# Perceiver block on one core: keys' chain between the query projections, queries' chain between the levels

## What is computed

```python
x = x + xattn(layernorm(x), ctx)
x = x + attn(layernorm(x))
x = x + ffn(layernorm(x))
```

```python
q, k, v = (silu(short_conv(h @ W.T, conv)) for q, k, v)
beta = sigmoid(h @ Wb.T)
q, k = q / |q|, k / |k|                 # per token and head
T = inverse(I + tril(beta * k @ k.T, -1))
delta = tril(q @ k.T) @ (T @ (beta * v))
o = p0 * fir3(v) + p1 * fir15(v) + p2 * fir63(v) + p3 * delta + p4 * v
return rmsnorm(o) @ Wo.T                # p0..p4: gate softmax per head
```

## Time and profile before

| | us |
|---|---|
| runs | 483.11, 485.64, 489.86 |
| median | 485.64 |
| the profiled execution | 488.1 |
| its span, first to last instruction | 486.3 |

### The profile page before, as it was taken

How to read it: one execution, slowest core, us unless ns; L and a number is a source line. 1 busy time by engine, 2 the same in 40 slices (tenths; PEclk the granted TensorE clock), 3 DMA queues, 4 the chain that set the end, 5 groups by cost and what they waited for, 6 DMA issues and landing times.

```text
span 486.3 us, 8120 instructions
## 1 busy us (share of the span) xinstructions
PE 447.0 (92%) x3154; PEld 291.8 (60%) x3154; DVE 317.7 (65%) x596; ACT 164.3 (34%) x208; POOL 78.6 (16%) x77
## 2 busy tenths in 40 slices
PE   2998997899998997899999979999998899999985
PEld 1953343445563574658776437887445688888862
DVE  5441225467983889997748774552214999999955
ACT  1102110245730010112223153204005788788630
POOL 1000000000004580002552110047200000000061
PEclk9999998899998599999968999999999999999998
DMA  8999939433040505007300020037707999999535
GB/s 324 430 427 427 425 137 306 156 81 93 1 173 19 156 21 157 3 1 276 160 3 0 2 86 0 1 128 223 235 1 292 375 402 395 373 410 405 219 112 169
DMA packets 17937, 92.41 MB, mean 190 GB/s; under 512 B 3424, under 2 KB 5104, under 8 KB 10736
## 3 DMA queue, kind: packets, MB, share of 16 engines
q1 hardware_dynamic: 14880, 78.82, 42.9%
q10 hardware_dynamic: 1488, 8.93, 5.3%
q0 software_dynamic: 1536, 4.20, 2.6%
HBM read 82.25 MB, written 12.08 MB: 194 GB/s over the span
## 4 chain that ended last, share of the span: by engine, by line
PE 77%; DVE 17%; issue 2%; ACT 1%; POOL 1%; DMA 1%; SPq 0%; DVEq 0%; ACTq 0%
PE bank L832 33%; PE bank L673 7%; PE bank L608 5%; PE bank L641 5%; PE bank L494 3%; PE bank L554 3%; PE bank L533 3%; PE bank L511 3%; DVE ring L1354 3%; DVE part L1354 3%; PE bank L809 3%; PE bank L657 2%; PE bank L658 1%; POOL small L415 1%; DVE ring L1443 1%
## 5 line engine op out<-in xcount | busy, mean ns | idle before, releaser
L608 PE MATMUL bank<-xnT,ring 128*128 128x512 f32 x96 | 44.8, 617 | 0.7 <-ACT xnT L971 0.7
L1354 DVE SCALAR_TENSOR_TENSOR part<-ring,cols,part 128x504 f32<-128x504 f32 (+13 forms) x64 | 42.7, 728 | 0.1
L673 PEld LDWEIGHTS bank<-ring 64*64 64x64 f32 x960 | 33.3, 140 | 14.0 <-issue 13.0
L673 PE MATMUL bank<-ring 64*64 64x64 f32 (+1 forms) x960 | 37.7, 231 | 2.9 <-issue 2.7
L641 PE MATMUL bank<-early,ring 128*32 128x512 f32 (+15 forms) x512 | 35.0, 420 | 1.4 <-DVE early L1377 1.4
L415 POOL TENSOR_TENSOR small<-small 128x1 f32<-128x1 f32 (+2 forms) x11 | 11.3, 1024 | 154.1 <-DVE small L1234 78.9
L1354 DVE SCALAR_TENSOR_TENSOR ring<-bank,cols,ring 128x504 f32<-128x504 f32 (+2 forms) x36 | 26.4, 733 | 14.2 <-ACT ring L1019 13.2
L608 PEld LDWEIGHTS bank<-xnT,ring 128*128 128x128 f32 x96 | 18.3, 197 | 21.8 <-issue 20.9
L641 PEld LDWEIGHTS bank<-early,ring 128*32 128x32 f32 x512 | 14.3, 114 | 18.1 <-issue 12.8
L1083 ACT ACTIVATE ring<-bank 128x256 f32<-128x256 f32 x20 | 7.7, 384 | 50.6 <-PE bank L673 50.2
L1125 ACT ACTIVATE rows<-bank 128x512 f32<-128x512 f32 x19 | 11.4, 598 | 36.0 <-PE bank L832 36.0
(11 more groups left out here) (245 smaller groups left out, 905.5 us busy)
## 6 DMA issues: line engine op xcount, KB each, us to landing
early<-wffn_in SPq DMA_DIRECT2D x21, 1024.0 KB, 7.4
ring<-ctxT_in SPq DMA_DIRECT2D x4, 2048.0 KB, 26.2
ring<-ctx_in SPq DMA_DIRECT2D x4, 2048.0 KB, 30.6
raw1b<-wffn_in SPq DMA_DIRECT2D x6, 1024.0 KB, 9.8
raw3b<-wffn_in SPq DMA_DIRECT2D x6, 1024.0 KB, 7.3
raw2b<-wffn_in SPq DMA_DIRECT2D x6, 1024.0 KB, 7.9
ring<-firw_in SPq DMA_DIRECT2D x4, 1024.0 KB, 5.5
xs<-zeros_in ACTq DMA_DIRECT2D x1, 3840.0 KB, 14.0
```

Source lines behind the costliest of these rows:

```text
L608: last = pe.matmul(bank[5 + g % 3][:, :], wqkv[:, j, c, h * P:(h + 1) * P], xnT[:, c, :], start=(c == 0), stop=(c == DC - 1))
L673: last = pe.matmul(dst[s, d], left[s, L * t:L * (t + 1)], right(s, t), start=True, stop=True)
L1354: return dve.scalar_tensor_tensor(out=d, in0=s, scalar=w, in1=d, op0=ALU.mult, op1=ALU.add)
```

## The change

- TensorE: the sums of squares are taken four planes at a time (`sum_rows`, `turn_sums`), for keys and for queries apart. The turns of v, the FIR rounds 0 to 7 of head 0, the keys' sums and the keys' table stand between the query projections; rounds 8 to 15 between the key factors and products. Rounds 10 to 15 of head 1, the query table, query factors and query scores stand in the steps of the first pair's levels. Six `keep_warm` matmuls are gone. Projections go to banks 1, 5 and 6, so that 7 is free for the FIR.
- ScalarE: takes the first tap of both short filters (8 instructions) and the scaling of v (16 instructions of 128x128) from VectorE.
- VectorE: asks for powers twice, 16 columns each; small loops over tiles are one instruction each; 20 of 64 taps stand in the projections, 44 in the levels; query factors and score masks stand between the updates.
- GpSimd: two powers of 16 columns; the masks of the second pair's levels 2, 3 and 4 stand behind the first pair's end and between the branch sums.
- SP: filters are loaded into three places instead of two; the load for head 0 stands ahead of the copies for head 1, the load for head 2 ahead of the copies of head 2.

The core of the diff (pieces of GpSimd, TensorE, ScalarE and VectorE in this order):

```diff
+            power(2 * NT + 1, 0, 16)
...
+            level_masks(0, 0)
+            level_masks(0, 1)
+            power(2 * NT + 2, 16, 16)
+            for l in range(2, NLV):
+                level_masks(0, l)
+            level_masks(1, 0)
+            level_masks(1, 1)
+            pool.wait_ge(S["tt_upd"], 2 * NLV - 1)
+            level_masks(1, 2)
...
+                if h < 2:
+                    level_masks(1, 3 + h)
...
+            def sum_rows(k):
+
+                pe.wait_ge(S["sq_done"], H * (k + 1))
+                for i in range(H):
+                    last = pe.matmul(bank[4][CG * i:CG * (i + 1), :], ones[:, 0:1].broadcast_to([P, CG]), sq_b[:, i, :],
+                                     start=True, stop=True)
+                last.then_inc(S["cols_done"], 1)
+
+            def turn_sums(k):
+
+                pe.wait_ge(S["cols_kept"], 2 * k + 1)
                 for t in range(NT):
-                    last = pe.matmul(bank[4][:, 256 + NT * i + t:257 + NT * i + t], sq_b[:, i % 2, t * P:(t + 1) * P],
-                                     ones[:, 0:1], start=True, stop=True)
+                    last = pe.matmul(bank[4][:, 16 * k + t:16 * (k + 1):NT], sum_row[:, t * P:(t + 1) * P],
...
-                    last = pe.matmul(bank[5 + g % 3][:, :], wqkv[:, j, c, h * P:(h + 1) * P], xnT[:, c, :],
+                    last = pe.matmul(bank[QB[g % 3]][:, :], wqkv[:, j, c, h * P:(h + 1) * P], xnT[:, c, :],
...
-                if g >= H + 2:
-                    sumsq(g - H - 2)
-            for h in range(H):
-                pe.wait_ge(S["silu_done"], h + 1)
-                if h == 2:
-                    keep_warm(bank[2][:, :], 4)
+                if 2 * H - 1 <= g < 3 * H - 1:
+                    turn_v(g - 2 * H + 1)
+                if g == 2 * H:
+                    fir_rounds(0, 0, 4)
+                    sum_rows(0)
+                if g == 2 * H + 1:
+                    turn_sums(0)
+                if g == 2 * H + 2:
+                    fir_rounds(0, 4, 8)
+                    turn_table(1, 3, 20, 24)
...
+            def key_factor(h):
+
                 if h >= 2:
-                    pe.wait_ge(S["bv_ready"], h - 1)
-                for t in range(NT):
-                    last = pe.transpose(bank[h % 2][:, t * P:(t + 1) * P], vP[:, h, t * P:(t + 1) * P], ident)
-                last.then_inc(S["vt_done"], 1)
...
+                    pe.wait_ge(S["kq_ready"], h - 1)
+                spread(bank[1 + 2 * (h % 2)][:, :], ct_k, h).then_inc(S["kq_done"], 1)
...
-            pe.wait_ge(S["conv_done"], 3 * H)
...
             pe.wait_ge(S["ct_lo"], 1)
...
-            for h in range(H):
-                coefficient(h, H * NPROB + h)
+            pe.wait_ge(S["conv_done"], 3 * H - 2)
+            key_factor(0)
+            key_factor(1)
+            fir_rounds(0, 8, 10)
+            key_factor(2)
+            key_factor(3)
+            fir_rounds(0, 10, 12)
...
-                pe.wait_ge(S["kq_ready"], h + 1)
+                pe.wait_ge(S["kq_ready"], min(h + 1 + 2 * (h % 2), H))
...
-            for h in range(2):
-                coefficient(H + h, h * NPROB + 3)
-            fir_rounds(1, 0, FW // 2)
-            for h in range(2, H):
-                coefficient(H + h, h * NPROB + 3)
-            for h in range(H):
...
-            fir_rounds(1, FW // 2, FW)
-            pe.wait_ge(S["kq_ready"], 2 * H)
-            for h in range(H):
+
...
                 if h == 3:
-                    pe.wait_ge(S["t1_ready"], H)
-                    keep_warm(bank[3][:, :], 2)
                     pe.wait_ge(S["at_ready"], 1)
...
+            fir_rounds(0, 12, FW)
+            sum_rows(1)
+            fir_rounds(1, 0, 6)
+            turn_sums(1)
+            first_transposes(0)
+            first_transposes(1)
+            fir_rounds(1, 6, 10)
+            first_transposes(2)
+            first_transposes(3)
...
             def between_first(step):
 
-                fir_rounds(2 + step // NLV, FW * (step % NLV) // NLV, FW * (step % NLV + 1) // NLV)
+                if step == 0:
+                    fir_rounds(1, 10, 13)
+                if step == 1:
+                    fir_rounds(1, 13, FW)
+                if 2 <= step < 6:
+                    fir_rounds(2, 4 * (step - 2), 4 * (step - 1))
+                if step >= 6:
+                    fir_rounds(3, 4 * (step - 6), 4 * (step - 5))
+                if step == 2:
+                    turn_table(2, 4, 0, H * NPROB)
+                if step in (4, 5):
+                    pe.wait_ge(S["ct_lo"], 2)
+                    query_factor(2 * step - 8)
+                    query_factor(2 * step - 7)
+                if step == 6:
+                    query_scores(0)
+                    query_scores(1)
+                if step == 7:
+                    query_scores(2)
+                if step == 8:
+                    query_scores(3)
...
-                    i = g - H
-                    act.wait_ge(S["silu_done"], g + 1)
-                    if i >= 2:
-                        act.wait_ge(S["sumsq_done"], i - 1)
-                    act.activation(sq_b[:, i % 2, :], plane[j][:, h], ACT.Square).then_inc(S["sq_done"], 1)
-
+                    act.activation(sq_b[:, h, :], plane[j][:, h], ACT.Square).then_inc(S["sq_done"], 1)
+                else:
+                    for medium, last_tap in ((0, KS - 1), (1, KS + KM - 1)):
+                        w = C_FIR + h * (KS + KM) + last_tap
+                        act.activation(branch[medium][:, h], vP[:, h], ACT.Copy,
+                                       scale=cols[:, w:w + 1]).then_inc(S["tap0_done"], 1)
...
+            def keep_sums(k):
...
+                act.wait_ge(S["cols_done"], 2 * k + 1)
+                act.activation(sum_row, bank[4][:, :], ACT.Copy).then_inc(S["cols_kept"], 1)
...
+            def scale_values(h):
+
+                act.wait_ge(S["vt_done"], h + 1)
+                for t in range(NT):
+                    ts = slice(t * P, (t + 1) * P)
+                    ins = act.activation(bv[:, h, ts], bank[2 * (h % 2)][:, ts], ACT.Copy, scale=beta[:, t, h:h + 1])
+                ins.then_inc(S["bv_ready"], 1)
...
+                if g == 2 * H + 1:
+                    keep_sums(0)
+                if g == 3 * H - 1:
+                    keep_table(0, ct_k, 3)
                 lag0(g)
                 silu(g - 1)
...
+                if g >= 2 * H:
+                    scale_values(g - 2 * H)
...
-            act.wait_ge(S["xT_done"], 2 * NT)
             keep_fir(0)
-            act.wait_ge(S["ct_done"], 1)
-            act.activation(ct[:, 0, :], bank[3][0:24, :], ACT.Copy).then_inc(S["ct_ready"], 1)
-            keep_fir(1)
+            keep_sums(1)
...
+                    if pair == 0 and l == 1:
+                        keep_fir(1)
...
+                    if pair == 0 and l == 1:
+                        keep_table(1, ct_q, 4)
...
-                for t in range(NT):
-                    g3 = gt[:, t, :].rearrange("p (h n) -> p h n", h=H)
-                    do(dve.tensor_tensor(g3, g3, itemp.unsqueeze(2).broadcast_to([P, H, NPROB]), ALU.mult))
+                do(dve.tensor_tensor(gt4, gt4, per_head(itemp), ALU.mult))
...
-                for t in range(NT):
-                    g3 = gt[:, t, :].rearrange("p (h n) -> p h n", h=H)
-                    do(dve.tensor_tensor(g3, g3, epsm.unsqueeze(2).broadcast_to([P, H, NPROB]), ALU.mult))
-                    do(dve.tensor_tensor(g3, g3, epsc.unsqueeze(2).broadcast_to([P, H, NPROB]), ALU.add))
+                do(dve.tensor_tensor(gt4, gt4, per_head(epsm), ALU.mult))
+                do(dve.tensor_tensor(gt4, gt4, per_head(epsc), ALU.add))
...
-                if g >= H:
-                    fir_taps(2 * (g - H), 2 * (g - H) + 2)
-                if g == 2 * H + 2:
-                    clear_heads(0)
-                if g == H + 1:
-                    gating_1()
-                if g == H + 2:
-                    gating_2()
-                if g == H + 3:
-                    gating_3()
-            for h in range(H):
-                dve.wait_ge(S["vt_done"], h + 1)
-                dve.tensor_tensor(bv[:, h].rearrange("p (t n) -> p t n", t=NT),
-                                  bank[h % 2][:, :].rearrange("p (t n) -> p t n", t=NT),
-                                  beta[:, :, h:h + 1].broadcast_to([P, NT, P]), ALU.mult).then_inc(S["bv_ready"], 1)
-            dve.wait_ge(S["sumsq_done"], 2 * H)
-            after(dve, dve.tensor_scalar(rs_in[:, 0:32], bank[4][:, 256:288], 1e-6, None, ALU.add), S["pow_wanted"])
-            clear_heads(1)
-            rsqrt(ktr, 0, 32)
...
+            def want_powers(k):
+
+                dve.wait_ge(S["sumsq_done"], k + 1)
+                cs = slice(16 * k, 16 * (k + 1))
+                dve.tensor_scalar(rs_in[:, cs], bank[4][:, cs], 1e-6, None, ALU.add).then_inc(S["pow_wanted"], 1)
...
-            for t in range(NT):
```

(73 more changed lines are left out.)

184 lines of the change are left out of this document (101 added, 83 removed).

## The result

The changed kernel takes 472.57 us (median of 470.66, 471.44, 473.71 and 473.73). The kernel before, on the same chip, takes 487.61 (485.64 was the median of three runs; a fourth took 489.57). The ratio is 0.971, 95% interval 0.965 to 0.977: faster by 2.9%. Some executions of a kernel are in a slower state, and all ratios here leave these out, so a ratio is not exactly the quotient of two medians. The profiled execution took 471.44, its span is 469.6, its mean granted clock 0.979 (before 486.3 and 0.965), so the spans differ by 16.7 us.

The account below looks back on a forecast made before the run. TensorE's own program sets the pace nearly everywhere. 23.5 us gained before the levels, 7.0 given back in them, 1.2 kept back: 488.1 - 15.3 = 472.8, or 470.4 on the median's scale; range 463 to 480, about 8 in 10.

Parts of the forecast that it names:

- Stretch one: From the first projection to the first level, 97.9 us before: levels start 23.5 us earlier.
- Moved into the levels: Query coefficients, FIR rounds 10 to 15 of head 1 and score matmuls leave the stretch before the levels: 8.4 us.
- Clock: Before the levels, FIR 1.5, key products 1.6 and key coefficients 0.6 us regained at full clock: 3.7 if TensorE stays fed.
- The new wait: Before the levels, TensorE waits 1.3 us for the query sums, whose last convolution begins about 147.1 on VectorE.
- The levels: First pair's levels, 36.00 us before: TensorE's work 39.9 plus waits 3.1 makes 43.0, giving back 7.0 us.
- Hand-overs: Semaphores of about ten new hand-overs between engines, set to zero in the sum: 1.2 us kept back for them.
- The clock does not come back: Rival, chance 0.13: without filling matmuls the clock stays low behind new waits; gain 8 to 9 us, about 477.
- VectorE is the bound: Rival, chance 0.15: VectorE's order stalls in the first pair's levels, ending 3 to 5 us later; about 474.
- It does more: Rival, chance 0.10: the second pair's clock dip vanishes too or new waits are smaller; gain 20 us, about 465.
- It does not do what it says: Rival, chance 0.05: a wait written for the wrong step serialises keys behind queries as before; 484 us.
- Slower: Rival, chance 0.04: clock stays at 0.50 from the interleaved stretch through the levels; 493 us with 30 us of such work.
- Exclusion for a whole instruction: GpSimd and two-SBUF-input VectorE operations exclude each other: in the levels the second update 1.5 us later, sum 15.0 instead of 16.5.

Follow-up runs that it names:

- e7: Kernel before without its six filling matmuls between the projections and the first level: 488.97 us, ratio 1.006 to the kernel before.
- e11: Changed kernel with the keys' 16-column power computed twice by GpSimd: 484.64 us, ratio 0.979 to the kernel before, on another chip.
- e6: Changed kernel with the keys' power, table, low half and scalings moved behind the last convolution, sums left in place: 482.51 us, ratio 0.989 to the kernel before.
- e8: Kernel before with only ScalarE's part of the change, eight first taps and the value scalings: 486.29 us, ratio 1.000 to the kernel before.
- e2: Changed kernel with the second step's four taps ahead of VectorE's first update: 466.08 us, ratio 0.962 to the kernel before.
- e12: Changed kernel with GpSimd's ten masks held back until both updates of level 0 are done: 482.02 us, ratio 0.974 to the kernel before.
- e9: e5 with two taps of the sixth step moved to the seventh: 475.28 us, ratio 0.958 to the kernel before, on another chip.
- e4: Changed kernel with the queries' chain put back ahead of the levels: 480.25 us, ratio 0.988 to the kernel before.
- e5: e2 with the clearing of head 2's stack one place earlier on VectorE: 468.45 us, ratio 0.963 to the kernel before.

## Why the prediction was right, point by point

- **Stretch one, 23.5 forecast, 24.1 measured.** *Idle:* the forecast was 3.9 less a new wait of 1.3; measured were 3.92 before and 1.02 + 0.67 after. The 0.67, ahead of the keys' sums at 128.33 where the last key's square is late, I had not foreseen. *Filling matmuls:* none is left, and e7 shows in what sense the 5.5 us count: without the cover, taking them out brings nothing. *Sums of squares:* by starts, L618 and L626 take 1.00, 0.81, 0.88 and 0.99, together 3.7 for 3.6, so 3.2 saved for the 3.3 of the sum. *Moved into the levels:* by starts, FIR rounds 1.4, table 0.5, factors 2.2, scores 4.2: 8.3 for the 8.1 by which TensorE's work was to grow there. *Clock:* key products 3.68 to 2.09; the FIR of heads 0 and 1, 8.93 and 9.26, now sums to 8.4 and 8.1.
- **The power.** Half of 5.43, 2.7, was a guess between two bounds; it took 2.91. "A convolution covers all but 0.5": VectorE waited 0.84. e11 shows that TensorE has little beyond that. "If that cover were gone the old 5 us would be back": in e6 VectorE waits 3.02 for the power, but TensorE's waits come to 8.6, since table, low half and first factor stand without cover too.
- **The new wait** stands where the prediction put it, for the last query's squares: 1.02 for 1.3. The convolution ahead of it began at 148.55, for 147.1 plus the 1.24 by which all ran late.
- **ScalarE.** A 128x128 copy with a factor took 0.28 (4 in 1.12), for 0.3. e8 shows what its place is worth: the same scalings in a row behind the projections hold TensorE for 2.4 us.
- **The levels, 7.0 given back forecast, 8.1 measured.** The waits were right as a sum, 3.1 for 44.04 - 41.09 = 2.95, and in place: 2.60 for the 2.0 at level 1's second head, behind the taps under masks (e2, e12). TensorE's work grew by 9.3 instead of 8.1. That is the term that was too small, and about 1.4 of it is half clock behind that very wait (48 matmuls 2.83, for 1.61 in e11 behind the same wait at full clock, and FIR 3.54 for 3.32). The prediction took full clock in the levels; a wait of 2 us should have carried a chance of that price.
- **VectorE in the levels.** Forecast were 42.8 us of work, measured 38.03. The prediction counts 3.1 twice: L1443 of the earlier trace rows ran until 188.5, so all of it behind 185.4 was in the 35.3 already. And four taps (2.60 at 158.77) now run ahead of the first level. That leaves 37.1, and 39.1 with the 2.0 that the masks cost the taps. TensorE did set the pace, as forecast, but VectorE had more room than the prediction gave it.
- **SP.** Head 3's stack was issued from 167.49 (forecast 166.7) and cleared at 184.01 (forecast 182.9), with no wait for it.
- **Hand-overs.** The reserve of 1.2 stands for no row. By the two stretches the change brought 24.1 - 8.1 = 16.0, between the 16.5 without it and the 15.3 with it. The spans differ by 16.7, since +1.24 at the start and -2.0 at the end came along, which are no part of the change; the medians of one chip differ by 15.0. That this meets the forecast of 15.2 (485.64 - 470.4) to 0.2 us is partly luck, since one program's runs here differ by 3.
- **The rivals.** *The clock does not come back:* this was true in a small part. Between projections and levels the clock was 1.00, where the rival had it low; a new short dip came behind the one long wait, and the one in the second pair stayed at 7 to 14 us. The Trainium skill, "TensorE: Matmul & The Clock Gate", section "What's actually happening", says that an idle array is throttled. e6 and e7 agree: 17 us at 0.50 about a wait of 7.21, and 10.2 about one of 4.01 that was filled before. e11 shows a wait of 2.60 at full clock. The dip at 232 does not follow from it: TensorE is busy for 39.87 of 39.93 us there. *VectorE is the bound:* it was not, with 38.03 of 44.04, but its order cost 2.6. *It does more:* it did not by itself; e9 shows that some 4 us were there to be had in the levels. *It does not do what it says:* it does, by the rows above. *Slower:* no run shows a clock that stays low through the levels.
- **Exclusion for a whole instruction.** "The first taps would wait for the second power": they did not, and took 0.65 each while GpSimd's power ran from 158.93 to 162.24. Beside masks both sides are slow and go in step: taps start every 1.09 us and so do the four masks beside them, where alone taps start every 0.62 and masks every 0.68. A 16-column operation beside masks starts every 0.68 too, at the masks' own pace. So the rule of the Trainium skill, "SBUF — State Buffer", section on two separate sides, fits this trace nearly for the masks (1.09 a pair, where strictly by turns it would be 1.30) and not for the power, and the sum by it (15.0) was rightly left.

## What to carry to other kernels

A chain of small steps over four engines is worth its waits, and the low clock behind them on top, when it can be put under work of TensorE: undoing either of two such covers cost 7 to 10 us here by the medians, and how the gain divides between them is open. When a chain moves, list what stands in order behind it on the busiest helper engine; what sets the wait may be a cheap operation (a clearing of 0.48 us behind six small ones) or taps that could as well stand in an idle gap ahead. Give a wait like the one of 2.60 us a chance of half clock behind it (about 1.4 us in the changed kernel, nothing in e11); behind the waits of 1.02 us there was none. And compare stages, not only medians: low clock outside the change moved a run by 3 us, as much as some of these edits.

## What was not expected of the hardware

- One kernel's executions differ by the length of a half-clock stretch while TensorE is busy without a gap: 6.8 us in 231 to 238 in one, 13.6 in 231 to 245 in the next, 3.0 us of span in all. What sets its length, and why some executions (e2, e4, e5, e7, e9, e12) had no low clock at 76 to 93 but one at 37 to 44, in a part of the program that is the same in all, is open.
- GpSimd's power costs by the column (2.91 us for 16, 5.43 for 32) and slows none of VectorE's taps; its masks of 128x256 do, 0.65 to 1.14, and lengthen even an operation on 16 columns from 0.17 to 0.65.
- Such a mask took 0.72 beside an idle VectorE and beside updates that read PSUM (the first six behind the second power), and 1.13 beside taps (the last four of that row).
- The profile's releaser for the 2.60 us wait (GpSimd's masks) was wrong; moving the taps on VectorE removed the wait with the masks where they were (e2).
- The same wait of 2.60 us had a low clock behind it in four kernels and none in e11, and e12 waited 3.15 without one.
